# Mixture-of-experts tail: the low halves of layer 1's weights at fixed addresses, and one expert number per tile

## The chip, the core and the metric

The kernel runs on one core of a Trainium2 chip. Five engines with queues of their own take part: TensorE (PE, matrix products; its weight loads are shown apart as PEld), VectorE (DVE), ScalarE (ACT), GpSimd (POOL), and SyncE (SP), which issues most of the DMA. Each engine has a sequencer that reads its instructions, works on registers and hands the rest to the engine. The metric is device microseconds of one execution. A difference of 0.3% (2 us here) is about what timing this kernel can tell from no change.

## The reference, cut to what matters

`x` is 32 sequences of 128 tokens with 256 features. First comes an attention-like layer with decay gates, added to `x`. Then a mixture of eight experts, two for each token:

```
scores = softmax(xf @ gate_w); the two largest are kept and divided by their sum
h = gelu(xf @ w1[e] + b1[e])          # 256 -> 1024, layer 1
y = h @ w2[e] + b2[e]                 # 1024 -> 256, layer 2
x = x + sum over the two experts of score * y
```

Only the two chosen experts of a token are computed here. All matrix products of the experts are done in float16 halves: a float32 value is a high half plus a low half, and of the four products three are summed.

## The kernel before

The attention steps write each token's normed row into a table in device memory, sorted by expert. The expert part then works on this table in 39 tiles. Tiles 0 to 31 have 256 rows; the last seven, tiles 32 to 38, have 128 rows: `NBIG` is 32, `NT` is 39, and `Turn.rows` gives the row count. Which expert a tile belongs to is only known on the chip: the list `exi` in SBUF (`ctx_slots` in the trace) holds one number for each tile, and each engine reads it into a register with `value_load`. Weights of all experts stay in SBUF in `w1s` (`w1_halves`; the trace leaves numbers out and writes `w_halves`): for each expert a high part (index 0) and a low part (index 1), each 2 x 1024 values in every partition. An address inside them depends on the register.

The work is written out by hand, in program order for each engine. PE's order is `tile_turn`. Turn t loads two expert numbers (`expert_of(t - 1)` and `expert_of(t)`), waits for the rows of tile t (`s_xh`), transposes the rows of tile t + 1 (`turn_rows`, L1504), runs layer 1 of tile t (L1519), and then layer 2 of tile t - 1 (L1533). Layer 1 has eight slices of 128 hidden features, in four quarters. A slice takes six matmuls: the high weight part times both halves of the rows, for two blocks of 128 input features (four matmuls, two for each weight block), and the low weight part times the rows' high half (two matmuls). A small tile's matmul has 128 columns. Layer 2 of a small tile has 24 matmuls of 256 columns.

Around it, ACT applies gelu as each quarter of layer 1 is done (L1038). DVE, in turn t, splits the rows of tile t + 1 into halves (`split_rows`, L2087 and L2089), computes their row numbers and gates (`row_fields`), splits the gelu of tile t into halves (`split_gelu`, four times L2096 and L2098), and at the end of the turn adds the bias and multiplies by the gate for tile t - 1 (`gate_rows`, L2105 and L2111). POOL adds these rows into the output with an indirect DMA (`add_rows`, L663) and waits for it to land before it goes on. SP loads the rows of tile t + 4 as soon as those of tile t have been used (`turn`, `load`). Turns 13 to 28 are a hardware loop; from turn 29 on every turn is written out (`late_turns`).

Of the kernel before, what the change touches and what calls it, by code (L numbers as in the profile page):

```python
# [9 lines left out]
F16 = mybir.dt.float16  # L10
# [3 lines left out]
P = 128  # L14
# [33 lines left out]
def build(nc, x, ctx_in, igate_w, igate_b, fgate_w, fgate_b, out_w, gate_w, w1, b1, w2, b2, out):  # L48
# [3 lines left out]
    HG = P // DH  # L52
    KC = D // P
    NE, _, F = w1.shape
    FC = F // P
    SB = 4
    NSTEP = NB // SB
# [6 lines left out]
    NT = (2 * T + NE * (R - 1)) // R  # L64
    NBIG = 2 * T // R
# [6 lines left out]
    LOOP_TURNS = (NBIG - 3) // 4  # L72
# [27 lines left out]
    with ExitStack() as ctx:  # L100
        def sb(name, shape, dt=F32):
            return ctx.enter_context(nc.sbuf_tensor(name, shape, dt))

        def sem(name):
            return ctx.enter_context(nc.semaphore(name))


        w1s = sb("w1_halves", [P, NE, 2, KC, F], F16)
# [4 lines left out]
        xres = xbuf[:, 1, :, :]  # L113
        ctxb = sb("ctx_slots", [P, SB, D])
        xfn = sb("xf_rows", [P, 2, SB, ROW])
# [44 lines left out]
        def listed(n):  # L160
            list_at[0] += n
            return ctxb[:, :, :].rearrange("p j d -> p (j d)")[:, list_at[0] - n:list_at[0]]

        rowi, exi, lim, rev = (listed(NT) for n in range(4))
        rowi, exi = rowi.bitcast(I32), exi.bitcast(I32)
# [7 lines left out]
        xT = sb("xf_halves_turned", [P, 2, SB, KC, P], F16)  # L173
# [142 lines left out]
        s_xf = sem("xf_ready")  # L316
        s_xo = sem("x1_written")
# [4 lines left out]
        s_lg = sem("logits_ready")  # L322
# [39 lines left out]
        v_last = vaug[:, 1, :, :, :].rearrange("p j h e -> p (j h e)")  # L362
        yo = [v_last[:, b * 2 * D:(b + 1) * 2 * D].rearrange("p (b d) -> p b d", d=D) for b in range(2)]
        yo += [work[:, 2 * b:2 * b + 2, :] for b in range(2)]
        ps_xt = ps_t
        ps_y = (ps_h, ps_m)
        FQ = FC // 4
# [7 lines left out]
        s_l1 = sem("layer1_quarter")  # L375
# [5 lines left out]
        s_y = sem("rows_gated")  # L381
        s_add = sem("rows_added")
        s_af = sem("scatter_ids_free")


        L20, Y0, FREE0 = 1, 4, 3
# [20 lines left out]
        def late_turns(eng, turn):  # L407
            with eng.Fori(LOOP_FIRST, LOOP_TURNS) as i:
                for u in range(1, 5):
                    turn(Turn(i, u), False, NT)  # L410
            for t in range(4 * LOOP_TURNS + 1, NT + 1):
                turn(Turn(0, t), False, NT - t)

        with nc.Block() as block:

            @block.sync
            def _(sp):
# [46 lines left out]
                def write_x1(step):  # L464
                    g = number(step)
                    sp.wait_ge(s_x1, g + 1)
                    sp.sem_inc(s_held, 1)
                    sp.dma_start(out_dram[g], xres[:, :, :]).then_inc(s_xo, 16)
# [51 lines left out]
                def load(tr, ahead):  # L520
                    k = tr.slot(ahead)
                    row = sp.value_load(rowi[0:1, bass.ds(tr.t + ahead, 1)], min_val=0, max_val=PAD_ROW)
                    sp.dma_start(xg[k], table[bass.ds(row, R), :].rearrange("(b p) w -> p b w", p=P)).then_inc(
                        s_gx[k], 16)

                def next_rows(t):
                    tr = Turn(0, t)
                    sp.wait_ge(s_xT, t + 1)
                    sp.wait_ge(s_id, t + 1)
                    load(tr, 4)  # L530

                def turn(tr, first, left):
                    if left > 4:
                        sp.wait_ge(s_xT, tr.t + 1)
                        sp.wait_ge(s_id, tr.t + 1)
                        load(tr, 4)

                write_x1(NEXT_LAST)
                sp.wait_ge(s_tl, 2)
# [26 lines left out]
                sp.wait_ge(s_clear, 16 * (NE + 1))  # L566
                for n in range(EARLY - 4, EARLY):
                    next_rows(n)
                late_turns(sp, turn)
                sp.wait_ge(s_xo, 16 * NSTEP)  # L570

# [534 lines left out]
            def _(pe):  # L1106
# [393 lines left out]
                def turn_rows(tr, ahead):  # L1500
                    pe.wait_ge(s_gx[tr.slot(ahead)], tr.landed(ahead))
                    for c in range(KC):
                        for b in range(tr.rows(ahead) // P):
                            ins = pe.transpose(ps_xt[:, c * R + b * P:c * R + b * P + P],  # L1504
                                               xg[tr.slot(ahead)][:, b, c * P:(c + 1) * P], ident[:, :])
                    ins.then_inc(s_xT, 1)

                def layer1(tr, expert, first, quarters=range(4)):

                    for f in range(quarters[0] * FQ, (quarters[-1] + 1) * FQ):  # L1510
                        if f % FQ == 0 and not first:
                            pe.wait_ge(s_ge, tr.t * 4 + (f // FQ - 3))
                        o = ps_s[:, f // FQ, (f % FQ) * R:(f % FQ) * R + tr.rows(0)]
                        n = 0
                        for a, parts in ((0, (0, 1)), (1, (0,))):
                            for k in range(KC):
                                w = w1s[:, bass.ds(expert, 1), a, k, f * P:(f + 1) * P].rearrange("p a f -> p (a f)")
                                for b in parts:
                                    ins = pe.matmul(o, w, xh[:, tr.slot(0) % 2, b, k, 0:tr.rows(0)], start=(n == 0),  # L1519
                                                    stop=(n == 3 * KC - 1))  # L1520
                                    n += 1
                        if f % FQ == FQ - 1:
                            ins.then_inc(s_l1, 1)

                def layer2(tr, expert, quarters=range(4)):
                    k = tr.slot(-1)
                    for f in range(quarters[0] * FQ, (quarters[-1] + 1) * FQ):
                        if f % FQ == 0:
                            pe.wait_ge(s_hh, tr.t * 4 + (f // FQ - 3))
                        for n, (a, b) in enumerate(HALVES):  # L1530
                            w = w2s[:, bass.ds(expert, 1), b, f, :].rearrange("p a d -> p (a d)")
                            for c in range(tr.rows(-1) // P):
                                ins = pe.matmul(ps_y[k % 2][:, c * D:(c + 1) * D],  # L1533
                                                hh[k % 2][:, a, f, c * P:(c + 1) * P], w,
                                                start=(f == 0 and n == 0 and c == 0),
                                                stop=(f == FC - 1 and n == 2 and c == tr.rows(-1) // P - 1))
                    if quarters[-1] == 3:
                        ins.then_inc(s_l2, 1)

                def expert_of(t):  # L1540
                    return pe.value_load(exi[0:1, bass.ds(t, 1)], min_val=0, max_val=NE - 1)

                def tile_turn(tr, first, left, beside=()):
                    beside = iter(tuple(beside) + (None,) * 8)

                    def routing():
                        op = next(beside)
                        if op is not None:
                            op[0](*op[1:])

                    if not first:
                        previous = expert_of(tr.t - 1)
                    if left > 0:
                        expert = expert_of(tr.t)
                        pe.wait_ge(s_xh, tr.t + 1)
                        if left > 1:
                            turn_rows(tr, 1)
                        for q in range(4):
                            layer1(tr, expert, first, (q,))
                            routing()  # L1560
                    if not first:
                        pe.wait_ge(s_y, tr.t * 2 + (Y0 - 4))
                        for q in range(4):
                            layer2(tr, previous, (q,))
                            routing()

                pe.sem_inc(s_l2, L20)
                sixth, last = NEXT_LAST, LAST
                scores(last, 3)
# [5 lines left out]
                stream_before(last, 3, 3)  # L1575
                times_v(last, 3)
                tile_turn(Turn(0, 0), True, NT, ((turn_xf, sixth, 0), (xf_left, sixth, 0), (turn_xf, sixth, 1)))
                pe.wait_ge(s_hev, NSTEP * SB)
                pe.wait_ge(s_mld, NSTEP)
                tile_turn(Turn(0, 1), False, NT, ((xf_left, sixth, 1), (logits, sixth)))  # L1580
                tile_turn(Turn(0, 2), False, NT, (None, (ranks, sixth)))
                tile_turn(Turn(0, 3), False, NT)
                tile_turn(Turn(0, 4), False, NT, ((turn_xf, last, 0), (xf_left, last, 0), (turn_xf, last, 1),
# [613 lines left out]
```

## Time and profile before

| what | value |
|---|---|
| timed runs | 666.69 us median of 3 (665.88 to 667.96) |
| span of the profiled execution | 672.2 us |
| TensorE busy in that span | 626.9 us (93%) |
| VectorE busy | 489.8 us (73%) |
| ScalarE busy | 323.3 us (48%) |
| mean granted TensorE clock | 0.981 |

The profiled execution has no other time on record than its span, from its first to its last instruction; the span is 5.5 us longer than the median of the timed runs. Durations below come from this one execution. A busy time counts modelled matmul durations, so a row of matmuls that overlap is read by the starts of its members, not by their lengths.

### The profile page before, as it was taken

The page shows a single profiled execution, that of the slowest core. Times are in us where ns is not written, and L with a number is a line of the kernel's source. Part 1 is how long each engine was busy: PE and PEld are TensorE (multiplying, and loading weights), DVE is VectorE, ACT ScalarE, POOL GpSimd, SP SyncE. Part 2 cuts the span into 40 slices and gives each one's busy share as a digit, 9 for nine tenths or more (in the row PEclk, how much of TensorE's full clock was granted, in tenths as well). Part 3 has the DMA queues.
Part 4 walks back from the last instruction along what each step waited for, and adds up shares of the span by engine and source line. Part 5 has one row for each costly group of instructions (what it writes and reads, how often), then busy time and mean ns, then how long its engine had stood idle before and what let it go on. Part 6 is the DMA issues. An engine that isn't in the chain of part 4 may idle for free. (4 is left out here: it accounts for less than half of the span.)

```text
span 672.2 us, 20373 instructions
## 1 busy us (share of the span) xinstructions
PE 626.9 (93%) x6736; PEld 533.2 (79%) x6737; DVE 489.8 (73%) x1330; ACT 323.3 (48%) x767; POOL 187.1 (28%) x185
## 2 busy tenths in 40 slices
PE   1799998999889899999999999999999999999985
PEld 1567876778677668988989898988889898988774
DVE  2457988979889898985889866757675757666562
ACT  2668888777878746543332232323232323232321
POOL 3000003231323315135345332313141323233112
PEclk9899999969999999999999999999999999999998
DMA  4534537654644636333374423233232323133100
GB/s 139 156 106 148 160 94 231 188 189 144 207 152 137 199 103 208 77 70 78 66 221 93 68 40 61 43 56 46 46 52 44 57 39 64 35 65 53 21 4 1
DMA packets 55036, 66.55 MB, mean 99 GB/s; under 512 B 5472, under 2 KB 50720, under 8 KB 54832
## 3 DMA queue, kind: packets, MB, share of 16 engines
q1 hardware_dynamic: 41552, 48.13, 24.1%
q0 software_dynamic: 13296, 17.32, 14.1%
q8 instruction: 49, 0.80, 0.5%
q14 instruction: 27, 0.22, 0.1%
q10 hardware_dynamic: 112, 0.08, 0.1%
HBM read 41.50 MB, written 24.92 MB: 99 GB/s over the span
## 5 line engine op out<-in xcount | busy, mean ns | idle before, releaser
L1038 ACT ACTIVATE decay_slots<-scores,b_turned 128x256 f32<-128x256 f32 (+1 forms) x312 | 124.4, 451 | 257.4 <-PE scores L1519 244.9
L1519 PE MATMUL scores<-x_slots,w_halves 128*128 128x256 f16 (+1 forms) x1872 | 203.3, 264 | 0.8 <-issue 0.8
L1519 PEld LDWEIGHTS scores<-x_slots,w_halves 128*128 x1872 | 173.4, 98 | 23.3 <-issue 1.4
L641 POOL DMA_INDIRECT expert_rows<-xf_rows,slot_i x64 | 66.7, 1042 | 224.1 <-issue 114.8
L1533 PE MATMUL pv<-w_halves,decay_slots 128*128 x864 | 97.7, 273 | 0.0
L663 POOL DMA_INDIRECT out_rows<-v_centred_and_one,row_ids x36 | 57.8, 1605 | 138.8 <-DVE v_centred_and_one L2111 96.1
L1533 PE MATMUL gate_bank<-w_halves,q_and_k_halves 128*128 x840 | 95.0, 273 | 0.0
L1533 PEld LDWEIGHTS pv<-w_halves,decay_slots 128*128 128x128 f16 x864 | 84.1, 98 | 10.5 <-issue 0.3
L1533 PEld LDWEIGHTS gate_bank<-w_halves,q_and_k_halves 128*128 128x128 f16 x840 | 81.8, 98 | 10.1
L663 POOL DMA_INDIRECT out_rows<-work,row_ids x35 | 55.3, 1580 | 112.1 <-DVE work L2111 84.7
L1257 PEld LDWEIGHTS pv<-v_centred_and_one,decay_slots 128*128 128x128 f32 x512 | 64.5, 197 | 1.6
L1257 PE MATMUL pv<-v_centred_and_one,decay_slots 128*128 128x33 f32 x512 | 64.7, 262 | 0.0
L2098 DVE TENSOR_TENSOR decay_slots<-decay_slots 128x512 f16<-128x512 f32 (+1 forms) x80 | 51.2, 640 | 2.7
L2098 DVE TENSOR_TENSOR q_and_k_halves<-decay_slots,q_and_k_halves 128x512 f16<-128x512 f32 (+1 forms) x76 | 49.5, 652 | 2.6
L1705 DVE SCALAR_TENSOR_TENSOR w_halves<-weight_stage,w_halves 128x1024 f16<-128x1024 f32 x32 | 38.9, 1219 | 10.5 <-ACT w_halves L780 10.3
L768 ACT ACTIVATE decay_slots<-turn_bank 128x512 f32<-128x512 f32 x64 | 38.2, 597 | 10.7 <-PE turn_bank L1153 9.5
L1714 DVE SCALAR_TENSOR_TENSOR decay_slots<-scores,decay_slots 128x1024 f32<-128x1024 f32 x32 | 39.1, 1222 | 4.6 <-PE scores L1200 3.2
L2087 DVE CAST x_slots<-turn_bank 128x512 f16<-128x512 f32 (+1 forms) x39 | 25.1, 643 | 17.9 <-PE scores L1519 10.2
L1255 PE MATMUL pv<-minus_big_above,ident_bf 128*128 128x240 bf16 x128 | 34.9, 273 | 2.7 <-ACT work L789 1.6
L2096 DVE CAST decay_slots<-decay_slots 128x512 f16<-128x512 f32 (+1 forms) x80 | 33.5, 419 | 5.1 <-ACT decay_slots L1038 4.0
L780 ACT ACTIVATE w_halves<-weight_stage 128x1024 f16<-128x1024 f32 x32 | 33.7, 1055 | 3.4 <-DMA weight_stage<-in_L_ffn_w 3.4
L2096 DVE CAST q_and_k_halves<-decay_slots 128x512 f16<-128x512 f32 (+1 forms) x76 | 32.4, 426 | 1.2 <-ACT decay_slots L1038 0.8
(257 smaller groups left out, 845.5 us busy)
## 6 DMA issues: line engine op xcount, KB each, us to landing
weight_stage<-in_L_ffn_w SPq DMA_DIRECT2D x32, 512.0 KB
x_slots<-in_x SPq DMA_DIRECT2D x16, 512.0 KB
weight_stage<-expert_rows SPq DMA_DIRECT2D x30, 272.0 KB
ctx_slots<-in_ctx SPq DMA_DIRECT2D x8, 512.0 KB
out_rows<-x_slots SPq DMA_DIRECT2D x8, 512.0 KB
v_centred_and_one<-expert_rows SPq DMA_DIRECT2D x9, 272.0 KB
expert_rows<-v_centred_and_one SPq DMA_DIRECT2D x9, 272.0 KB
expert_rows<-xf_rows,slot_i POOLq DMA_INDIRECT x64
```

Source lines behind the costliest of these rows:

```text
L641: pool.indirect_dma_start(table, bass.IndirectOffsetOnAxis(ap=sloti[:, step[1], j, k:k + 1], axis=0), xfn[:, step[1], j, :], None, bounds_ ...
L663: pool.indirect_dma_start(out_rows, bass.IndirectOffsetOnAxis(ap=ids[:, k, b:b + 1], axis=0), yo[k][:, b, :], None, bounds_check=T - 1, oo ...
L768: act.activation(E[:, j, HG * r:HG * r + HG, :].rearrange("p c s -> p (c s)"), ps_t[:, :], ACT.Exp).then_inc(s_ee, 1)
L1038: ins = act.activation(hf[:, f * R:f * R + tr.rows(0)], ps_s[:, q, n * R:n * R + tr.rows(0)], ACT.Gelu, bias=b1T[:, bass.ds(expert, 1), f] ...
L1255: pe.matmul(ps_h[:, P + P + 16:512], ident_h[:, :], never[:, 0:120].unsqueeze(1).broadcast_to([P, 2, 120]), start=True, stop=True)
L1257: ins = pe.matmul(ps_h[:, h * (DH + 1):(h + 1) * (DH + 1)], E[:, j, k * KC + u, :], vaug[:, step[1], j, h, :], start=True, stop=True)
L1519: ins = pe.matmul(o, w, xh[:, tr.slot(0) % 2, b, k, 0:tr.rows(0)], start=(n == 0), stop=(n == 3 * KC - 1))
L1533: ins = pe.matmul(ps_y[k % 2][:, c * D:(c + 1) * D], hh[k % 2][:, a, f, c * P:(c + 1) * P], w, start=(f == 0 and n == 0 and c == 0), stop= ...
L1705: dve.scalar_tensor_tensor(out=lo, in0=stage[:, half, :], scalar=W_SCALE, in1=hi, op0=ALU.mult, op1=ALU.subtract).then_inc(s_lo, 1)
L1714: dve.scalar_tensor_tensor(out=c, in0=ps_s[:, :, 0:KC * P], scalar=QK_SCALE, in1=c, op0=ALU.mult, op1=ALU.mult).then_inc(s_cm, 1)
L2096: dve.tensor_copy(hi, src).then_inc(s_hhi, 1)
L2098: dve.tensor_tensor(lo, src, hi, ALU.subtract).then_inc(s_hh, 1)
```

## The change

From the small tiles on, the low part of layer 1's weights is not read from `w1s` through the register, but from one of four places that do not depend on the expert (`w1_low`). They lie in buffers that the attention steps no longer need: two in `xfn` (`xf_rows`), one in `xres` (`x_slots`), one in `xT` (`xf_halves_turned`). SP copies 512 KB there from `w1s` for each small tile (`copy_low`): in turn 29 for tile 32, and so on to turn 35 for tile 38. The fifth to seventh copy wait until layer 1 of the tile that used the place before is done. PE waits for the copy (`s_wl`) ahead of layer 1. Before its loop SP gets three waits for the end of the earlier use of these buffers.

The second part: from turn 30 on PE no longer loads two expert numbers at the head of a turn. It keeps the number in a Python variable, that is, in the register, and loads only the next tile's (`coming`), after the third quarter of layer 2.

```diff
@@ SP
+                def copy_low(m):
+                    if m >= NLOW:
+                        sp.wait_ge(s_l1, (NBIG + m - NLOW + 1) * 4)
+                    expert = sp.value_load(exi[0:1, NBIG + m:NBIG + m + 1], min_val=0, max_val=NE - 1)
+                    sp.dma_start(w1_low[m % NLOW], w1s[:, bass.ds(expert, 1), 1, :, :].rearrange(
+                        "p a k f -> p (a k) f")).then_inc(s_wl[m % NLOW], 16)
+
                 def turn(tr, first, left):
...
                         load(tr, 4)
+                    m = tr.t - (4 * LOOP_TURNS + 1) if isinstance(tr.t, int) else -1
+                    if 0 <= m < NT - NBIG:
+                        copy_low(m)
...
+                sp.wait_ge(s_xo, 16 * NSTEP)
+                sp.wait_ge(s_xf, SB * NSTEP)
+                sp.wait_ge(s_lg, NSTEP)
                 late_turns(sp, turn)
@@ PE, layer1
+                    m = tr.t - NBIG if isinstance(tr.t, int) else -1
+                    if m >= 0 and quarters[0] == 0:
+                        pe.wait_ge(s_wl[m % NLOW], (m // NLOW + 1) * 16)
...
-                                w = w1s[:, bass.ds(expert, 1), a, k, f * P:(f + 1) * P].rearrange("p a f -> p (a f)")
+                                if a and m >= 0:
+                                    w = w1_low[m % NLOW][:, k, f * P:(f + 1) * P]
+                                else:
+                                    w = w1s[:, bass.ds(expert, 1), a, k, f * P:(f + 1) * P].rearrange("p a f -> p (a f)")
@@ PE, tile_turn
-                    if not first:
-                        previous = expert_of(tr.t - 1)
+                    nonlocal previous, expert, coming
+                    held = isinstance(tr.t, int) and tr.t > 4 * LOOP_TURNS + 1
+                    if held:
+                        previous, expert = expert, coming
+                    else:
+                        if not first:
+                            previous = expert_of(tr.t - 1)
+                        if left > 0:
+                            expert = expert_of(tr.t)
                     if left > 0:
-                        expert = expert_of(tr.t)
...
                             layer2(tr, previous, (q,))
                             routing()
-
+                            if q == 2 and left > 1 and isinstance(tr.t, int) and tr.t > 4 * LOOP_TURNS:
+                                coming = expert_of(tr.t + 1)
```

What PE's program holds at two places, first in layer 1 of a small tile. One slice before (ISA is the register step that makes the next weight address, `x2` two matmuls in a row):

```order
L1519 ISA
L1519 MATMUL scores<-x_slots,w1_halves 128x128 x2
L1519 ISA
L1519 MATMUL scores<-x_slots,w1_halves 128x128 x2
L1519 ISA
L1519 MATMUL scores<-x_slots,w1_halves 128x128
L1519 ISA
L1519 MATMUL scores<-x_slots,w1_halves 128x128
```

The same slice of the changed kernel, where `xf_rows` is one of the four fixed places:

```order
L1545 ISA
L1545 MATMUL scores<-x_slots,w1_halves 128x128 x2
L1545 ISA
L1545 MATMUL scores<-x_slots,w1_halves 128x128 x2
L1545 MATMUL scores<-x_slots,xf_rows 128x128 x2
```

Two of the four register steps of a slice are gone; the six matmuls are the same.

The second place is the border between two turns of small tiles on PE. Before, from the last matmuls of layer 2 to the first of layer 1:

```order
L1533 ISA
L1533 MATMUL pv<-w2_halves,decay_slots 128x256 x2
L1541 TENSOR_LOAD ctx_slots
L1541 ISA x2
L1541 TENSOR_LOAD ctx_slots
L1541 ISA x2
L1504 MATMUL turn_bank<-ident,weight_stage 128x128 [waits rows_in1,row_halves]
L1504 MATMUL turn_bank<-ident,weight_stage 128x128
L1519 ISA [waits gelu_quarter]
```

In the changed kernel, from the last matmuls of layer 2's third quarter on; two rows that repeat the fourth quarter's slice are left out:

```order
L1559 MATMUL pv<-w2_halves,decay_slots 128x256 x2
L1567 TENSOR_LOAD ctx_slots
L1567 ISA x2
L1559 REGISTER_ALU [waits gelu_halves]
L1559 MATMUL pv<-w2_halves,decay_slots 128x256
L1559 ISA
...
L1559 MATMUL pv<-w2_halves,decay_slots 128x256 x2
L1525 MATMUL turn_bank<-ident,weight_stage 128x128 [waits rows_in1,row_halves]
L1525 MATMUL turn_bank<-ident,weight_stage 128x128
L1545 ISA [waits gelu_quarter,w1_low_copied0]
```

One load remains, six matmuls ahead of the border, and the wait for the copy stands at the first register step of layer 1. In layer 2 the first of a slice's two register steps has become a REGISTER_ALU. The programs of DVE, ACT and POOL are the same as before.

## Rows read from the trace of the kernel before

**Rows 1.** TensorE in order of time, turns 32 to 39: start, us, line, count, idle before.

```profile
606.42 3.85 PE L1519 MATMUL scores<-x_slots,w_halves 128*128 128x128 f16 x48
610.27 5.41 PE L1533 MATMUL gate_bank<-w_halves,q_and_k_halves 128*128 x48
615.52 0.38 PE L1504 MATMUL turn_bank<-ident,weight_stage 128*128 128x128 f32 x2
615.74 3.81 PE L1519 MATMUL scores<-x_slots,w_halves 128*128 128x128 f16 x48
...
623.24 0.41 PE L1504 MATMUL turn_bank<-ident,v_centred_and_one 128*128 128x128 f32 x2 [0.88 <-issue]
623.49 4.27 PE L1519 MATMUL scores<-x_slots,w_halves 128*128 128x128 f16 x48
627.76 2.81 PE L1533 MATMUL gate_bank<-w_halves,q_and_k_halves 128*128 x24
...
654.95 4.32 PE L1519 MATMUL scores<-x_slots,w_halves 128*128 128x128 f16 x48 [0.78 <-issue]
...
662.07 2.81 PE L1533 MATMUL pv<-w_halves,decay_slots 128*128 x24
```

**Rows 2.** What TensorE waited for, 606 to 665 us: in all, times, longest.

```profile
PE turn_bank L1504 <- issue: 2.8, 4, 0.9
PE scores L1519 <- issue: 0.8, 1, 0.8
```

**Rows 3.** TensorE and its sequencer (PEldq) by line, from 606 us on: count, ns min/median/max.

```profile
L1519 PE MATMUL scores<-x_slots,w_halves x336: 219/227/228, 606.4 to 659.0; 128*128 128x128 f16 x168
L1519 PEldq FUSED_REGOPS  x221: 46/46/51, 606.2 to 658.9; - x111
...
L1541 PEldq TENSOR_LOAD <-ctx_slots x13: 296/303/481, 613.6 to 661.2; - x13
L1541 PEldq FUSED_REGOPS  x13: 146/151/151, 613.9 to 661.6; - x13
```

**Rows 4.** TensorE in order of time, cut to three short stretches.

```profile
606.42 1.11 PE L1519 MATMUL scores<-x_slots,w_halves 128*128 128x128 f16 x17
...
623.87 3.76 PE L1519 MATMUL scores<-x_slots,w_halves 128*128 128x128 f16 x41
...
39.79 1.35 PE L1166 MATMUL gate_bank<-gate_w_halves,q_and_k_halves 128*128 128x16 f16 x48
```

**Rows 5.** GpSimd in order of time: adds of tiles 31 and 32, and the last two.

```profile
617.72 1.55 POOL L663 DMA_INDIRECT out_rows<-work,row_ids  x1 [5.91 <-DVE work L2111]
...
624.64 1.55 POOL L663 DMA_INDIRECT out_rows<-v_centred_and_one,row_ids  x1 [3.52 <-DMA out_rows<-work,row_ids]
...
663.91 1.55 POOL L663 DMA_INDIRECT out_rows<-v_centred_and_one,row_ids  x1 [5.98 <-DVEq L2116]
668.39 1.55 POOL L663 DMA_INDIRECT out_rows<-work,row_ids  x1 [2.92 <-DMA out_rows<-v_centred_and_one,row_ids]
```

**Rows 6.** VectorE in order of time, turns 33 and 34.

```profile
618.60 0.29 DVE L2096 CAST q_and_k_halves<-decay_slots 128x256 f16<-128x256 f32 x1
...
620.93 0.42 DVE L2098 TENSOR_TENSOR q_and_k_halves<-decay_slots,q_and_k_halves 128x256 f16<-128x256 f32 x1
622.52 0.42 DVE L2105 SCALAR_TENSOR_TENSOR v_centred_and_one<-pv,q_and_k_halves 128x256 f32<-128x256 f32 x1 [1.16 <-PE pv L1533]
...
625.44 0.35 DVE L2096 CAST decay_slots<-decay_slots 128x256 f16<-128x256 f32 x1
...
628.93 0.42 DVE L2098 TENSOR_TENSOR decay_slots<-decay_slots 128x256 f16<-128x256 f32 x1
```

**Rows 7.** Stretches of turns 33 and 37: PE, PEld, DVE, ACT, POOL busy, clock, DMA share, GB/s.

```profile
615.52:623.24 7.72, 6.84 (x76) 5.60 (x75) 5.77 (x19) 2.50 (x8) 3.10 (x2) 1.00 0.43 73
646.92:654.95 8.03, 7.24 (x74) 5.79 (x75) 5.05 (x16) 2.50 (x8) 1.55 (x1) 1.00 0.02 1
```

**Rows 8.** DMA issues: count, KB of one, median us from issue to landing.

```profile
q_and_k_halves<-in_L_ffn_b SPq DMA_DIRECT2D x1, 1024.0 KB, 6.4
```

More of the change, by code:

```diff
@@ L364, in build @@
         yo += [work[:, 2 * b:2 * b + 2, :] for b in range(2)]
+        low_homes = [xfn[:, :, :, :].rearrange("p a j w -> p (a j w)")[:, s * 1024:(s + 1) * 1024].bitcast(F16)
+                     for s in range(2)]
+        low_homes += [xres.rearrange("p j d -> p (j d)").bitcast(F16),
+                      xT[:, :, :, :, :].rearrange("p a j c t -> p (a j c t)")]
+        w1_low = [h.rearrange("p (k f) -> p k f", k=KC) for h in low_homes]
+        NLOW = len(w1_low)
         ps_xt = ps_t
@@ L383, in build @@
         s_af = sem("scatter_ids_free")
+        s_wl = [sem(f"w1_low_copied{n}") for n in range(NLOW)]
         L20, Y0, FREE0 = 1, 4, 3
@@ L1565, in tile_turn @@
                             routing()
+                            if q == 2 and left > 1 and isinstance(tr.t, int) and tr.t > 4 * LOOP_TURNS:
+                                coming = expert_of(tr.t + 1)
+                previous = expert = coming = None
                 pe.sem_inc(s_l2, L20)
```

## The prediction

> **What bounds the kernel now.** I read the stretch that the change touches, turns 32 to 39, first in TensorE's order of time [rows 1]. From the first matmul of tile 32's layer 1 (606.42) to the first of tile 38's layer 2 (662.07) it takes 55.65 us. TensorE is the engine that never waits for another one here: in its list of waits the only releaser is "issue", 3.6 us in all, five times, 0.8 us or so at each border between two small turns [rows 2]. "Issue" means that no engine, DMA or semaphore is late; the matmuls had not been handed over yet.
>
> So look at the sequencer. Its rows [rows 3] show 32 register steps in each layer 1 (221 recorded of 7 x 32), one for each new weight address, and for each expert number a load of 303 ns and a register step of 151 ns. Whether the steps or the array set the pace is seen in two cuts of the same line [rows 4]. At the start of tile 32's layer 1, where the sequencer is still ahead because a big layer 2 lies before it, 17 matmuls take 1.11 us. Less the length of the last one (0.219), that is 16 intervals of 55.7 ns. In tile 34, 41 matmuls take 3.76 us, 40 intervals of 88 ns. Same shape, same weights, same granted clock of 1.00, 2.4 GHz [rows 7]. A slice of six matmuls thus takes 6 x 55.7 = 334 ns where the array sets the pace, and 6 x 88 = 530 ns where four register steps do, 132 ns a step. Layer 1 of small tiles is bound by the sequencer, and so is the border, where it loads two numbers one after the other.
>
> A whole small turn confirms this: 48 register steps (32 in layer 1, 16 in layer 2) at 132 ns are 6.34 us, and two loads at about 0.78 make 7.9; the turns take 7.7 to 8.0 [rows 1, 7].
>
> What follows layer 2 of tile 37 is a chain of its own: its add is issued at 663.91, the last one waits until that has landed, 668.39, and the span ends at 672.2, all of it 10.1 us after 662.07 [rows 1, 5].
>
> **The register steps removed.** Layer 1 of the seven small tiles loses 16 of 32 steps. Per slice the sequencer then needs two steps, 264 ns, and hands over two matmuls with fixed addresses. What those cost bare, 48 matmuls with fixed operands show early in the kernel: 1.35 us, at most 28 ns each [rows 4]. Together 320 ns at most, below the array's 334. So I take 55.7 ns for all 48 matmuls, 2.67 us a layer; the other end is what the two undisturbed layers take now, 3.8 us.
>
> **The loads removed.** One load of two goes, the other moves ahead of layer 2's last quarter. Its bare length is 303 + 151 = 0.45 us; as a whole it costs the sequencer about 0.78, by the sum above. The new turn on the sequencer: 32 steps x 0.132 = 4.22, plus 16 fixed matmuls x 0.028 = 0.45, plus 0.78, together 5.45 us. On the array: 2.67, plus layer 2 at 5.25 / 48 = 0.109 us a matmul, 24 of them 2.63, plus the transposes 0.22 (615.52 to 615.74), together 5.52 [rows 1]. So the sequencer keeps up, with little to spare, and the idle time at the border goes; were it not covered, I would allow 0.3 us a turn. In turns 29 to 31 a load moves too; the big layer 2 hides it as it hides the two loads now, since no idle time stands at 606.42 or 615.52 [rows 1].
>
> **The sum on TensorE.** Turn 32: 2.67 + 5.25 + 0.22 = 8.14 us to the next layer 1, instead of 9.32. Turns 33 to 37: 5 x 5.52, less 0.22 since turn 38 has no transposes, 27.4. Turn 38: 2.67 + 2.63 = 5.30. In all 40.8 instead of 55.65: 14.8 us less.
>
> **What is late next.** VectorE. From the bias of tile 32 (622.52) to the first split of tile 34's gelu (625.44) it needs 2.92 us; the four splits, where nothing is waited for, take 618.60 to 621.35 in turn 33, 2.75 [rows 6]. That is 5.67 us a turn, slightly over TensorE's 5.52. Five turns lose 0.75, part of which the last turn wins back, having no rows to split. Where the splits wait for ScalarE, as in turn 34, they end at 629.35, and the path is 6.83; this is the other end, but ScalarE's wait there came from the slow layer 1. GpSimd: an add with its landing takes 663.91 to 668.39, 4.5 us [rows 5], less than a turn. Only tile 31, with two adds, is close: issued 617.72, free again for 624.64. VectorE waits for this before it computes the row numbers of tile 35, and does so 2.2 us sooner after it than now, since turn 33 is shorter by that.
>
> **The copies.** Seven of 512 KB. The nearest row is a transfer of 1024 KB, 6.4 us from issue to landing [rows 8]; so 3.2 to 6.4 us each. The first four are issued three turns ahead, in big turns of over 9 us. The copy for tile 36 starts when tile 32's layer 1 ends and is needed 8.14 + 3 x 5.52 - 2.67 = 22 us later; the next two have 19. Behind the waiting SP stands only the load of rows that are due three turns on. So they cost TensorE nothing; if that cover were gone, up to 6.4 us for each late copy. They do share the DMA engines, busy 0.43 of turn 33 [rows 7], with tile 31's adds: 0 to 3 us on GpSimd, once, passed to VectorE. The three waits of SP before its loop, at turn 13, are for work of the attention steps, the last of which PE has in its turns 4 and 5. PE's seven waits for copies ride on register steps, and the steps of layer 2 that become REGISTER_ALU I price like the others.
>
> I take 1.2 us off for VectorE, GpSimd and the load together (0 to 4 by the bounds): 13.6 us. The sum is made on the profiled span, 672.2; the timed median is 5.5 less, 0.8%, which on 13.6 us is 0.1. So 666.7 - 13.6 = **653.1 us**.
>
> **The rivals.**
>
> *VectorE or GpSimd becomes the bound.* If the path stays at 6.83 a turn, five turns give back 5 x (6.83 - 5.52) = 6.6 us: a gain of 8.2, 658.5 us. For it: the margin of VectorE is nil. Against: 5 us busy a turn, the rest being waits [rows 7].
>
> *The array itself can't go faster for long.* If 55.7 ns lasted only as long as weights had been loaded ahead, layer 1 would stay at 3.8 us, and only the idle 3.6 us and 5 x 0.4 us of layer 1 would go: 5.6 us, 661.1. Against: 17 in a row, and the break comes where the lead of the sequencer ends. The Trainium skill (TensorE: Matmul & The Clock Gate, "Back-to-back issue gap") has such a rule, about 81 ns a matmul at 128 columns in a stream of weight loads and matmuls. By that rule a layer would take 3.9 us and the time would be about 661; the 55.7 ns of this trace speak against it, on a short run.
>
> *Nothing changes.* The steps leave, but something unseen holds the turn at 7.9 us. No wait in TensorE's list bears that out: 666.7.
>
> *Slower.* The copies land late: SP issues them in one queue with the rows, and TensorE waits at layer 1 for a place that is not filled. The last three decide it: they would lose the whole gain where each landed about 5 us after its need, that is 24 to 27 us after its issue, 20 GB/s. Then three waits of some 6 us make 18 against 13.6: 671. Turn 33 moved 73 GB/s beside everything else [rows 7].
>
> **How the numbers follow.** Both stalls go, 652 to 656: 0.62. VectorE or GpSimd bound, 656 to 660: 0.20. Array, 661: 0.08. No change: 0.05. Slower: 0.05. The likeliest gives the time. The range takes in the first two, from a full 15 us (651.5) to a gain of 7 (659.7). Faster by over 0.3% is the first three, 0.90.
>
> **What would show it.** Right: layer 1 of small tiles as 48 matmuls in about 2.8 us, 16 steps each, no idle "issue" before L1504's successor, turns of 5.5 to 5.8 us, and VectorE with hardly any wait for TensorE. Wrong: 80 ns between matmuls with no register step between them; a wait for a copy ahead of layer 1; GpSimd waiting for a landing in turns 34 to 36 with VectorE behind it.

## The result and the profile after

The changed kernel takes 649.99 us (median of 4 runs, 649.25 to 651.1) against 666.72 us for the kernel before (4 runs, 665.88 to 667.96): a ratio of 0.9752, with a 95% interval from 0.9718 to 0.9787. It is 16.7 us faster; 13.6 were forecast, and the range ended 1.5 us above the measured time.

| | before | after |
|---|---|---|
| span of the profiled execution | 672.2 us | 649.1 us |
| start of tile 32's layer 1 | 606.42 | 598.07 |
| from there to tile 38's layer 2 | 55.65 us | 40.81 us |
| from there to the end | 10.1 us | 10.26 us |
| mean granted TensorE clock | 0.981 | 0.986 |

The whole stretch that the change touches shrank by 14.8 us, to 40.81; the sum in the prediction had 40.8. The other 8.3 us of the difference between the two spans lie ahead of tile 32; they are taken up below.

TensorE in order of time, after (start, us, line, count), the answer to [rows 1]:

```profile
598.07 0.39 PE L1545 MATMUL scores<-x_slots,w_halves 128*128 128x128 f16 x4
598.29 0.28 PE L1545 MATMUL scores<-x_slots,xf_rows 128*128 128x128 f16 x2
598.40 0.39 PE L1545 MATMUL scores<-x_slots,w_halves 128*128 128x128 f16 x4
...
600.75 5.40 PE L1559 MATMUL gate_bank<-w_halves,q_and_k_halves 128*128 x48
605.99 0.38 PE L1525 MATMUL turn_bank<-ident,weight_stage 128*128 128x128 f32 x2
606.21 0.39 PE L1545 MATMUL scores<-x_slots,w_halves 128*128 128x128 f16 x4
...
608.89 2.78 PE L1559 MATMUL pv<-w_halves,decay_slots 128*128 x24
611.51 0.38 PE L1525 MATMUL turn_bank<-ident,v_centred_and_one 128*128 128x128 f32 x2
611.73 0.39 PE L1545 MATMUL scores<-x_slots,w_halves 128*128 128x128 f16 x4
...
638.88 2.78 PE L1559 MATMUL pv<-w_halves,decay_slots 128*128 x24
```

A slice of layer 1 is now two rows: four matmuls with the high weights through the register, then two with the low weights out of the copy (`xf_rows` here). From slice to slice it is 0.33 us (598.07 to 598.40), six matmuls at 55.7 ns, and eight slices take 2.68 us (598.07 to 600.75), where 3.8 to 4.3 stood in [rows 1]. No row carries an idle time in brackets, not even the transposes (L1525), and the list of waits from 597 to 650 us has no line for TensorE. The lines by which the sequencer had been recognised [rows 3] now read (line, count, ns min/median/max, from, to):

```profile
L1545 PE MATMUL scores<-x_slots,w_halves x224: 219/219/219, 598.1 to 636.1; 128*128 128x128 f16 x112
L1545 PEldq FUSED_REGOPS  x106: 46/46/51, 598.1 to 635.1; - x106
L1567 PEldq TENSOR_LOAD <-ctx_slots x6: 298/300/311, 602.7 to 631.5; - x6
```

106 register steps are recorded (of 7 x 16) in place of 221, 6 loads in place of 13. The stretches of the turns 32 to 35 and of turn 38, from layer 1 to layer 1 (columns as in [rows 7]), are 8.14, 5.52, 5.51, 5.52 and 5.31 us; the sum had 8.14, 5.52 and, for turn 38, 5.30:

```profile
598.07:606.21 8.14, 8.14 (x101) 7.58 (x99) 5.08 (x17) 2.50 (x8) 3.10 (x2) 1.00 0.52 116
606.21:611.73 5.52, 5.52 (x77) 5.25 (x75) 4.99 (x17) 2.50 (x8) 3.10 (x2) 1.00 0.35 62
611.73:617.24 5.51, 5.51 (x76) 5.25 (x74) 3.49 (x13) 2.50 (x8) 1.09 (x1) 1.00 0.73 224
617.24:622.76 5.52, 5.52 (x76) 5.25 (x74) 4.43 (x16) 2.50 (x8) 2.01 (x2) 1.00 0.19 45
...
633.57:638.88 5.31, 5.31 (x74) 5.03 (x72) 4.25 (x14) 2.50 (x8) 1.25 (x1) 1.00 0.04 5
```

TensorE is busy through the whole of each stretch at a granted clock of 1.00. The copies run beside it: the DMA engines' share rises to 0.73 and 224 GB/s in turn 34, with no mark on TensorE. From issue to landing a copy takes 3.1 to 4.1 us (DMA issues: count, KB, median us):

```profile
xf_rows<-w_halves SPq DMA_DIRECT2D x4, 512.0 KB, 4.1
x_slots<-w_halves SPq DMA_DIRECT2D x2, 512.0 KB, 3.1
xf_halves_turned<-w_halves SPq DMA_DIRECT2D x1, 512.0 KB, 4.1
```

### The profile page after: what moved, and what is told of

The parts are those of the page before. It is cut to its first block and busy times, and to the rows that moved or that the text cites. A ratio compares the mean times of both kernels' runs of the same rounds, so it can differ in the third digit from the quotient of the medians.

```text
span 649.1 us, 20273 instructions
## 1 busy us (share of the span) xinstructions
PE 611.4 (94%) x6736; PEld 526.6 (81%) x6737; DVE 487.2 (75%) x1330; ACT 323.4 (50%) x767; POOL 193.7 (30%) x185
## 3 DMA queue, kind: packets, MB, share of 16 engines
q0 software_dynamic: 13296, 17.32, 14.7%
## 5 line engine op out<-in xcount | busy, mean ns | idle before, releaser
L1545 PE MATMUL scores<-x_slots,w_halves 128*128 128x256 f16 (+1 forms) x1760 | 193.7, 266 | 0.0
L1545 PEld LDWEIGHTS scores<-x_slots,w_halves 128*128 x1760 | 165.2, 98 | 17.3
L662 POOL DMA_INDIRECT expert_rows<-xf_rows,slot_i x64 | 71.9, 1124 | 211.8 <-issue 107.0
```

The lines of the kernel that those rows point to most:

```text
L662: pool.indirect_dma_start(table, bass.IndirectOffsetOnAxis(ap=sloti[:, step[1], j, k:k + 1], axis=0), xfn[:, step[1], j, :], None, bounds_ ...
```

## The experiments

The first theory is that of the prediction: the sequencer paces the small tiles by its register steps and loads, so the two parts of the change act on one resource. Rivals were that one part gives everything, that the gain comes from elsewhere (it is 2 us above the stretch's own), and that VectorE has become the next bound.

All experiments compute the full output. In the table, the stretch runs from the first matmul of tile 32's layer 1 to the first of tile 38's layer 2, in the profiled execution of each kernel. The first four share 17 runs of the kernel before (median 666.02), the last three share 11 others (664.46).

| kernel | time, us (runs) | ratio, 95% interval | stretch | tile 32 starts |
|---|---|---|---|---|
| fixed places alone | 652.28 (6) | 0.9814 (0.9778 to 0.9850) | 44.11 | 599.19 |
| held number alone | 658.25 (6) | 0.9900 (0.9862 to 0.9937) | 49.03 | 599.96 |
| copies alone, unread | 669.38 (12) | 1.0048 (1.0019 to 1.0077) | 57.79 | 599.55 |
| the change once more | 652.26 (6) | 0.9801 (0.9755 to 0.9847) | 40.81 | 600.08 |
| two loads, early | 653.07 (2) | 0.9811 (0.9743 to 0.9880) | 42.83 | 595.28 |
| one load, at the head | 652.11 (2) | 0.9797 (0.9726 to 0.9868) | 40.81 | 602.54 |
| VectorE a turn ahead | 650.47 (6) | 0.9774 (0.9734 to 0.9814) | 40.81 | 595.01 |

### Fixed places alone

```diff
-                    if held:
-                        previous, expert = expert, coming
...
+                    if not first:
+                        previous = expert_of(tr.t - 1)
                     if left > 0:
+                        expert = expert_of(tr.t)
...
-                                coming = expert_of(tr.t + 1)
```

> The copies and the fixed addresses alone; TensorE loads two expert numbers at the head of each turn as before. If register steps set layer 1's pace, a small layer 1 takes 2.7 us or a little more, the idle time of some 0.8 us at each border of small turns stays, and a small turn is 6.2 to 6.3 us on the sequencer (32 steps x 0.132, 16 fixed matmuls x 0.028, two loads x 0.78): 10 to 11 us less than before. If the array can't keep 56 ns a matmul (the rival), layer 1 stays near 3.8 us and the gain is 2 us at most.

Measured: the stretch takes 44.11 us, 11.5 less than before, of 14.8 for the whole change; 10 to 11 were expected. Each layer 1 takes 2.68 to 2.73 us, 2.68 in the whole change, though two loads stand ahead of it again. What is lacking is the border (waits of TensorE, then the turns 36 and 37, columns as above):

```profile
PE turn_bank L1525 <- issue: 1.5, 4, 0.8
PE scores L1545 <- issue: 0.4, 1, 0.4
```

```profile
626.26:632.12 5.86, 5.74 (x77) 5.16 (x75) 4.44 (x16) 2.50 (x8) 1.55 (x1) 1.00 0.05 4
632.12:637.94 5.82, 5.47 (x74) 4.92 (x72) 4.67 (x16) 2.50 (x8) 1.55 (x1) 1.00 0.04 5
```

1.9 us of idle "issue" remain where 3.6 stood [rows 2]: the borders have shrunk although their loads are all there, since the sequencer now reaches them earlier. In the turns with no copy beside their loads 0.3 to 0.5 us are lost (turn 36 takes 5.86 for 5.52, turn 37, which has no transposes behind it, 5.82 for 5.30), near the 0.3 that the prediction allowed for a load that is not covered. Two turns with a copy in flight lose more: turn 32 takes 8.61 for 8.14, with loads of 564 and 1029 ns, and turn 34 takes 6.51 for 5.51, with one of 877 ns. The 6.2 to 6.3 us that were expected of a turn, by the prediction's prices, were too much: the turns 33, 35 and 36 take 5.98, 5.97 and 5.86.

### Held number alone

The kernel before, with the number kept and loaded once, and no copies:

```diff
+                    held = isinstance(tr.t, int) and tr.t > 4 * LOOP_TURNS + 1
+                    if held:
+                        previous, expert = expert, coming
...
+                            if q == 2 and left > 1 and isinstance(tr.t, int) and tr.t > 4 * LOOP_TURNS:
+                                coming = expert_of(tr.t + 1)
```

> The expert number held in the register and loaded once, one tile ahead; all weights through the register, no copies. If the sequencer sets the turn, a small turn is 48 steps x 0.132 + 0.78 = 7.1 us, without idle time at the borders but with layer 1 as slow as before: about 4 us less than before. If the borders' idle time were the main thing, the gain would be over 7 us.

Measured: 49.03 us, 6.6 less than before, where about 4 were expected; the turns 34 to 36 take 7.0 to 7.1, as expected. TensorE in order of time, the layer 1 of tiles 32 to 35:

```profile
599.96 2.89 PE L1519 MATMUL scores<-x_slots,w_halves 128*128 128x128 f16 x48
...
608.30 2.87 PE L1519 MATMUL scores<-x_slots,w_halves 128*128 128x128 f16 x48
...
614.23 4.12 PE L1519 MATMUL scores<-x_slots,w_halves 128*128 128x128 f16 x48
...
621.30 4.04 PE L1519 MATMUL scores<-x_slots,w_halves 128*128 128x128 f16 x48
```

The idle time at the borders is gone, and with no loads in its way the lead that the sequencer has from the big layers 2 lasts through two layers 1 (2.89 and 2.87 us for 3.85 and 3.81 in [rows 1]). Then it is used up, and layer 1 is back at 4.1: 32 steps of some 130 ns. The turns 32 and 33, with 8.34 and 5.93 us for 9.32 and 7.75, give 2.8 us of the 6.6, which the expectation did not have. 11.5 and 6.6 together are 18.1, more than the 14.8 of both: each part shortens the work of the same sequencer, and once both are in, TensorE's array sets the turn (5.52 us) and the rest of the saving has no effect. Two separate causes would have added up.

### Copies alone

As the first experiment, but `w` always comes from `w1s` through the register; the seven copies are made and waited for, and what they bring is not read.

```diff
-                                if a and m >= 0:
-                                    w = w1_low[m % NLOW][:, k, f * P:(f + 1) * P]
-                                else:
-                                    w = w1s[:, bass.ds(expert, 1), a, k, ...
+                                w = w1s[:, bass.ds(expert, 1), a, k, ...
```

> The seven copies, SP's three waits and TensorE's seven waits for the copies, but the copies are not read: weights and expert numbers as before. If the copies are hidden: within 1 us of before, no wait of TensorE for a copy. If they collide with row loads or with GpSimd's adds: up to 3 us slower, seen as a longer landing of the adds of tiles 31 to 33.

Measured: 0.5% slower than before, with a stretch of 57.79 us, 2.15 more. So the copies bring nothing by themselves, and have a price where the sequencer is the bound. The turns 35 to 37 take 0.09 us more than before with loads as before (296 to 312 ns). What they have more is one record on the sequencer: ahead of layer 1 there are two waits now, and one of them is a step of its own (L1535 EVENT_SEMAPHORE) and doesn't ride on a register step as the prediction had it. The rest stands in the turns 33 and 34, 1.1 and 0.7 us longer than before: 0.66 and 0.61 at the borders behind them, and 0.45 in turn 33's layer 1, behind a load of 677 ns. SP's issues, TensorE at the turns 34 and 35 and its loads of expert numbers from 614 to 625 us:

```profile
613.96 0.50 SPq L544 DMA_DIRECT2D xf_rows<-w_halves  x1
622.85 0.49 SPq L544 DMA_DIRECT2D x_slots<-w_halves  x1
```

```profile
617.56 0.41 PE L1525 MATMUL turn_bank<-ident,v_centred_and_one 128*128 128x128 f32 x2 [1.54 <-issue]
...
626.17 0.41 PE L1525 MATMUL turn_bank<-ident,weight_stage 128*128 128x128 f32 x2 [1.20 <-issue]
```

```profile
L1564 PEldq TENSOR_LOAD <-ctx_slots x3: 416/912/1155, 615.2 to 624.2; - x3
```

A load that takes 303 ns at the median [rows 3] took 1155 and 912 ns where it began 1.2 and 1.3 us after the issue of a copy, and the border behind it is idle for 1.54 and 1.20 us, instead of 0.88 [rows 1] and 0.59. The adds, which had been expected to land later, are not what TensorE waits for. In the whole change the same copies fly, but none of TensorE's six loads in small turns stands 1 to 2.4 us behind the issue of one, and they take 298 to 311 ns. Three earlier ones do, in the turns 29 to 31: they take 858, 486 and 634 ns, and TensorE has no wait there, since a big layer 2 covers them.

### The change once more, beside the parts

> The changed kernel once more, in more rounds. The stretch from tile 32's first layer 1 matmul to tile 38's layer 2 takes 40.8 us as before the repeat. If the 2 us by which the timed gain (16.7) exceeds the traced gain of that stretch (14.7) are differences between runs of code that did not change, the timed gain comes down towards 15 us, 651.5 to 652.5; if the change also shortens something else, it stays at 16 to 17 us, 650.

Measured: 652.26 us, 13.8 less than the kernel before in the same comparison, and a stretch of 40.81 us again. All seven starts of layer 1 have the same distances as in the first profile, to 0.01 us; tile 32 starts at 600.08 instead of 598.07. Of the two cases expected, this is the one in which the 2 us are differences between runs.

### Two loads, both early

```diff
-                        previous, expert = expert, coming
+                        previous, expert = (again if left > 0 else expert), coming
...
+                                again = expert_of(tr.t)
                                 coming = expert_of(tr.t + 1)
```

> The changed kernel, but TensorE loads two numbers (the held one again) at the early place, after the third quarter of layer 2. If what counts is the sequencer's total of a turn, this is as slow as two loads at the head with fixed addresses, 5.8 to 6.0 us a small turn, 43 to 44 us from tile 32's first layer 1 matmul to tile 38's layer 2. If what counts is the place of the load, both hide and the stretch stays at 40.8 us.

Measured: a stretch of 42.83 us, 2.0 more than the change, which neither end of the expectation met; turns of 5.7 to 5.95 us. Its loads and the waits of TensorE:

```profile
L1567 PEldq TENSOR_LOAD <-ctx_slots x12: 296/303/510, 599.9 to 631.3; - x12
```

```profile
PE pv L1559 <- DVE q_and_k_halves L2134: 0.4, 2, 0.2
PE gate_bank L1559 <- DVE decay_slots L2134: 0.4, 2, 0.2
PE pv L1559 <- issue: 0.2, 1, 0.2
```

The waits name VectorE's splits (L2134), but the split that this quarter of layer 2 needs had ended long before: for the first wait, which ends at 608.45, at 600.9. What stands right ahead of the waits is the second load. One load more costs 0.3 to 0.4 us in each of the turns 33 to 37, 2.0 in all. In the fixed places alone, with two at the head, it is 3.3 us, but 1.5 of this stand in the turns 32 and 34 with their loads beside a copy, and 1.8 in the others: the place changes little.

### One load, at the head of the turn

```diff
-                        previous, expert = expert, coming
+                        previous = expert
+                        if left > 0:
+                            expert = expert_of(tr.t)
...
-                                coming = expert_of(tr.t + 1)
```

> The changed kernel, but the one load stands at the head of the turn instead of six matmuls earlier. If the total counts, the sequencer has 0.3 us to spare in a turn and the stretch stays within 0.5 us of 40.8, but for turns 33 and 34, where a copy in flight can lengthen the load to about 1 us. If the place counts, idle time of 0.3 us or more stands at each border and the stretch is 42.5 us or more.

Measured: 40.81 us, the turns of the whole change to 0.01 us, and no wait of TensorE. The place of the load, "one tile ahead", gives nothing here; that it is one instead of two gives everything that this part of the change is worth. The longest of its six loads took 380 ns; it began 0.95 us after the issue of a copy.

### VectorE's number a turn ahead

VectorE still loads its own expert number at the head of each turn. Here it loads it behind the last split of the gelu, one turn ahead.

```diff
+                    elif isinstance(tr.t, int) and tr.t > 4 * LOOP_TURNS + 1:
+                        expert = ahead
...
+                        if isinstance(tr.t, int) and tr.t > 4 * LOOP_TURNS:
+                            ahead = start_of(tr.t)
```

> The changed kernel, and VectorE too loads its expert number a turn ahead, behind the last split, from turn 30 on. If VectorE's path of 5.7 us a turn and its load of 1.1 us beside a copy in turn 34 are what delays the last two biases, VectorE waits for TensorE in each small turn again, the stretch on TensorE stays at 40.8 us, and what follows the first matmul of tile 38's layer 2 shrinks from 10.2 to about 9.3 us; in the timed runs 0 to 1 us, within their spread. If GpSimd's chain of adds alone sets the end, it stays at 10.2 us.

Measured: the stretch is unchanged, and what follows it takes 10.58 us instead of 10.26: no gain at the end, where some had been expected (a tail of 9.3). In order of time on VectorE:

```profile
612.62 0.22 DVE L2109 SCALAR_TENSOR_TENSOR first_part<-v_centred_and_one,ctx_slots 128x2 f32<-128x2 f32 x1 [1.58 <-POOLq L689]
...
616.30 0.42 DVE L2140 SCALAR_TENSOR_TENSOR v_centred_and_one<-gate_bank,q_and_k_halves 128x256 f32<-128x256 f32 x1 [0.45 <-issue]
```

The load isn't hidden: behind the last split there is an idle 0.45 us "issue" ahead of the bias, since the sequencer takes the load up only when the split has begun: both start at 615.4, and the load takes 0.42 us, its register step 0.18. And what VectorE gained at the head of turn 34 it lost 1.58 us later, waiting for GpSimd's two adds of tile 31. Its time, 650.47 us, is not below that of the change by more than the two medians of the change itself differ.

## Where the prediction was right, and the steps that failed

The mechanism on TensorE came out as forecast: 40.81 us for 40.8. The time did not: 16.7 us of gain for 13.6, below the range. Two steps failed. The sum took 1.2 us off for a lag of VectorE, GpSimd and the load; the runs show 0 on TensorE and 0.1 us behind it. And it took all that lies ahead of tile 32 as equal in the two sets of runs, a term put at nothing without a reason; two medians of the same changed kernel are 2.3 us apart. The second has no part in the change. With the second median, 652.26, the time would have stood inside the range, so that it stood below is in part bad luck.

**The bound and the steps removed: right.** Layer 1 of small tiles was paced by the sequencer, and 48 matmuls at 55.7 ns are what it takes without that. The fixed places alone bring this about with two loads still there.

**The loads removed: right in effect, wrong in the margin.** Seven loads fewer in the stretch are worth 3.3 us beside the fixed places (44.11 to 40.81). The prediction had 5.45 us of sequencer against 5.52 of array, 0.07 to spare. With its price of 0.78 a second load would have made 6.23 us; measured, where no copy is beside the loads, are 5.86 to 5.98 in the turns 33 to 36, at the head as well as early. Where the sequencer is the bound, one load less took 0.8 us off a turn (7.84 on the mean of the turns 33 to 37 before, 7.0 held). So with one load the sequencer needs some 5.1 us, 0.4 less than the array; this is an estimate from these turns. It fits that a load at the head does no harm. For a turn with two loads the prices added up to some 0.3 us too much; which of them was too high was not taken apart. That the load stands a tile ahead was given no value of its own; the run with the load at the head shows it has none.

**The rival of the array: fell.** 336 matmuls, seven times 48, each with a weight load of its own, kept 55.7 ns. The rule of the Trainium skill (TensorE: Matmul & The Clock Gate, "Back-to-back issue gap"), about 81 ns for such a stream at 128 columns, does not hold here as a floor; what stood at 80 to 90 ns in this kernel were the sequencer's steps. Layers of 2.9 us without fixed addresses, in the held number alone, show the same: 2.89 less the last matmul's 0.22 is 47 intervals of 57 ns. So it was not the place that the weights are read from either.

**VectorE next: right, and without a price.** From bias to bias VectorE needs 5.67 us as worked out, and TensorE 5.52. In order of time on VectorE, the biases (L2140) of tiles 32 to 37, and the head of turn 34:

```profile
611.82 0.42 DVE L2140 SCALAR_TENSOR_TENSOR v_centred_and_one<-pv,q_and_k_halves 128x256 f32<-128x256 f32 x1
612.28 0.35 DVE L2146 TENSOR_SCALAR v_centred_and_one<-v_centred_and_one,row_gates 128x256 f32<-128x256 f32 x1
614.32 0.42 DVE L2122 CAST x_slots<-turn_bank 128x256 f16<-128x256 f32 x1 [1.69 <-PE scores L1545]
...
615.36 0.22 DVE L2109 SCALAR_TENSOR_TENSOR first_part<-v_centred_and_one,ctx_slots 128x2 f32<-128x2 f32 x1 [0.16 <-POOLq L689]
...
618.52 0.42 DVE L2140 SCALAR_TENSOR_TENSOR v_centred_and_one<-gate_bank,q_and_k_halves 128x256 f32<-128x256 f32 x1
...
624.23 0.42 DVE L2140 SCALAR_TENSOR_TENSOR work<-pv,q_and_k_halves 128x256 f32<-128x256 f32 x1
...
629.90 0.42 DVE L2140 SCALAR_TENSOR_TENSOR work<-gate_bank,q_and_k_halves 128x256 f32<-128x256 f32 x1
...
635.58 0.42 DVE L2140 SCALAR_TENSOR_TENSOR v_centred_and_one<-pv,q_and_k_halves 128x256 f32<-128x256 f32 x1
...
640.05 0.42 DVE L2140 SCALAR_TENSOR_TENSOR v_centred_and_one<-gate_bank,q_and_k_halves 128x256 f32<-128x256 f32 x1
```

The distances are 6.70, 5.71, 5.67, 5.68 and 4.47 us. Turn 34 is the long one: the wait of 1.69 us is put down to TensorE, but it holds VectorE's own load of the expert number, which took 1.14 us there, beside a copy. VectorE falls behind, from 0.42 us after the start of the last matmul of layer 2 to 2.1, without making TensorE wait, and catches up in the last turn, which has no rows to split. GpSimd's adds of tile 31, feared with 0 to 3 us, cost it 0.16.

**The term that was mis-sized: "1.2 us off for VectorE, GpSimd and the load together (0 to 4 by the bounds)".** It measured 0 on TensorE. In what follows the stretch it was 0.1 us (10.26 for 10.14; 10.12 in the repeat): the last bias is where it was, 2.9 us behind the stretch's end, and the last-but-one add, issued 2.84 us behind it instead of 1.84 [rows 5], is made up for by its sooner landing (GpSimd in order of time, after):

```profile
641.72 1.55 POOL L684 DMA_INDIRECT out_rows<-v_centred_and_one,row_ids  x1 [2.30 <-DVEq L2151]
...
645.36 1.55 POOL L684 DMA_INDIRECT out_rows<-work,row_ids  x1 [2.08 <-DMA out_rows<-v_centred_and_one,row_ids]
```

From issue to issue it is 3.64 us, against 4.48 [rows 5]. The error was to price a lag of VectorE's as time on the path, where the prediction itself had the last turn win part of it back. Without the term the sum gives a gain of 14.7 us, 652.0 us, which the second measurement (652.26) meets and the first (649.99) doesn't.

**The other 2 us: no part of the change.** The attention steps, hundreds of microseconds ahead of the first copy, run the same instructions in both kernels. Their length is not the same from run to run. In the two profiles most of the 8.3 us ahead of tile 32 can be located: between two issues of SyncE that are the same in both (at 135.2 and 203.4 us before, at 136.0 and 196.2 after) TensorE has 788 matmuls in both. This stretch of before and the 10 us from 138, and below, after (columns as in [rows 7]; the third last is the granted clock):

```profile
135.20:203.40 68.20, 62.52 (x788) 50.59 (x788) 57.52 (x164) 53.14 (x127) 18.36 (x20) 0.90 0.54 168
138.00:148.00 10.00, 10.00 (x47) 8.05 (x46) 6.24 (x15) 6.56 (x14) 4.67 (x6) 0.50 0.54 175
```

```profile
136.00:196.20 60.20, 56.11 (x788) 45.71 (x788) 56.62 (x164) 52.12 (x125) 21.48 (x20) 1.00 0.61 191
```

8.0 of the 8.3 us arise here. In the profile before, the granted clock stood at 0.50, 1.2 GHz, from 138 to 148 us, behind a wait of TensorE for ScalarE of 1.5 us, and again from 182 to 186, 13.7 us in all; in the profile after it was 1.00 throughout, 2.4 GHz. The same matmuls kept TensorE busy 6.4 us longer, and it was idle 1.6 us longer.

This belongs to that one execution. Its span of 672.2 us is longer than that of each of the 28 timed runs of the kernel before whose span is on record, 659.1 to 667.5. With 65.8 us from tile 32 to the end, as in the profile, those runs would start tile 32 between 593 and 602 us, an estimate; the changed kernel and the experiments start it between 595.0 and 602.5. So no run shows that anything ahead of tile 32 moved with the change. For the same reason the prediction's step from the span to the timed median, "5.5 less", set a long execution against shorter ones; where a run has both, its time is 2 to 3 us above its span.

Outside the end of the execution the lower level lasted 20.5 us before, 13.7 after, and between 6.8 and 23.9 in the experiments, and tile 32 started between 595.0 and 602.5 us in those, in this order at both ends. How long it lasted is not all: the held number alone has 20.5 us of it too, at other places, and starts tile 32 at 599.96. Of the timed runs, those with a mean granted clock of 0.986 had spans of 662.2, 662.5 and 664.0 us before, and 647.9 to 651.0 us after (6 runs): 13.7 us between the means, 662.9 and 649.2. At 0.989 it is 661.7 (2 runs) and 647.3 (1 run), 14.4. A straight line through the spans of the 28 runs before against their mean clock, and one with the same slope through the 10 of the changed kernel, lie 14.5 us apart (15.3 with the first four alone, 14.0 with the repeat's six). So at equal clock the change is worth about what the stretch lost, 14.7. That the clock alone made the first comparison 2 us more is not shown: its runs of the kernel before have no clock on record, and two sets of the changed kernel at 0.986 still differ by 1.6 us (648.4 and 650.0 on the mean).

**The range.** It was built from mechanisms alone. Medians of one kernel differ here by 2 us between comparisons (664.46 to 666.72 before, 649.99 to 652.26 after). A lower end of 651.5 (a full 15 us off 666.7 is 651.7), 0.5 us under the 652.0 of the full gain of 14.7, had no room for that.

**The chances.** "Both stalls go" had 0.62; what it describes came true, but the time that went with it, 652 to 656, holds the repeat's 652.26 and not the first 649.99. "Slower" needed copies that land 24 to 27 us after their issue: they land 3.1 to 4.1 us after it, at the lower end of the 3.2 to 6.4 forecast, and were issued turns ahead.

## What to carry to other kernels

When matmuls stand closer together in one place than in another, with the same shape and clock, count what the sequencer does between them: each address in a register has a step of its own, and halving these steps in layer 1 was worth 11.5 us here where no engine had been waited for. Two savings on one sequencer don't add up once the array sets the pace, and with a margin of some 0.4 us the place of what was left in the turn no longer mattered here. The one execution that is profiled stood some 8 us above the timed runs here, so compare its span with theirs. Before an engine's lag is priced, look whether anything waits for it before a turn comes in which it catches up.

## What was not expected of the hardware

A load of one number from SBUF into a register takes longer while a DMA copy inside SBUF is in flight. On TensorE's sequencer it took 1155 and 912 ns instead of 303 in the copies alone, on VectorE's 1139 ns in the change, and 1133 and 1125 ns in its repeat and in the one load at the head, each time in turn 34. VectorE's sequencer, after, in all small turns and then at the head of turn 34 alone (line, count, ns min/median/max, from, to):

```profile
L2158 DVEq TENSOR_LOAD <-ctx_slots x8: 300/304/1139, 599.0 to 641.0; - x8
```

```profile
L2158 DVEq TENSOR_LOAD <-ctx_slots x1: 1139/1139/1139, 612.8 to 612.8; - x1
L2158 DVEq FUSED_REGOPS  x1: 190/190/190, 614.0 to 614.0; - x1
```

The copy of that turn was issued at 611.3. All seven profiles with copies say the same. From the first copy on, 26 loads of TensorE and VectorE start 0.9 to 2.4 us after the issue of a copy: each of them took 368 ns or more, up to 1155. Of 136 that start earlier than that, or over 3.4 us after, all but one (510 ns) took 296 to 320; in between, both occur. The rows loaded for a tile, whose issue mostly stands 1.1 to 1.3 us ahead of the copy's, are not needed for it: the 912 ns began 1.3 us after a copy and 11.5 us after the last rows. ScalarE does not follow in the one case at hand: a load 1.2 us after a copy, with VectorE's number a turn ahead, took 274 ns. Without copies, in the kernel before, three of 35 such loads of TensorE and VectorE from 557 us on took 432 to 481 ns, so that other transfers may lengthen them too. What in the copy does it was not taken apart.

TensorE's matmuls and weight loads in the same stretches show no such effect: 5.51 us for turn 34, with the DMA engines at 0.73, and 5.52 for turn 35, at 0.19.
